# One core, four layers: the first layer's norm moves into its attention block, the first batch's experts move into the second batch, and the second layer's outputs go to two column groups

## The chip, the cores and the metric

The kernel runs on one core of a Trainium2 chip. The metric is the device time of one launch in microseconds (us); lower is better. The engines are TensorE (PE; PEld is its weight loading), VectorE (DVE), ScalarE (ACT), GpSimd (POOL) and SyncE (SP), which here only issues DMAs. Engines run their own instruction lists in order and meet at semaphores.

## The reference, cut to what matters

Eight batches of 512 tokens, 128 features, fp32, pass through four layers. Each layer is an attention-like mix followed by a feed-forward part. The change touches layers 0 and 1.

```
# layer 0: x -> norm -> xn; attention and experts both read xn, both are added to x
q, k = rms_norm(xn @ Wq, q_scale), rms_norm(xn @ Wk, k_scale)        # 16 heads of 8, mean over each head
attn = softmax(q @ k.T * hd ** -0.5);   o = (attn @ v) @ Wproj + bproj
logits = xn @ gate_w.T + gate_b                                      # 10 experts, 8 of them true
weights = top 2 of softmax(logits), null experts dropped, renormalised
y = sum over e of weights[e] * (xn @ expert_w[e]) + weights[e] * expert_b[e]

# layer 1: linear attention with decay, S_t = decay * S_(t-1) + k_t v_t, out_t = q_t S_t, then @ Wo.T + bo
# and experts chosen by a threshold of 0.9 on the summed probabilities, with a capacity per expert
```

## The kernel before, in words

Activations lie feature by token: `x` and `xn` are [128, 4096], batch b is the columns b*512 to b*512+511. Each part of a layer is one block, and a block ends with a barrier of all engines.

**The first norm** is a block of its own (`layer0_norm`, L306). SP loads the constants, `x` in two halves and the first weights. For each batch PE takes the mean (L225), DVE centres (L243), ACT squares (L254), PE takes the variance (L229), ACT takes logarithm and exponent for the reciprocal root (L258, L260) and DVE scales (L247). The attention block starts when all eight batches are normed.

**Layer 0's attention block** (`layer0_mix`, L396). A ring of three PSUM slots of two banks each (`ring_order0`) carries nearly all products; its order is that in which PE fills and others empty them. The code before the loop makes q and k of batch 0 (L745), their squares on POOL (L483), head means (L759) and roots on ACT (L492 to L500), scales and splits them on DVE (L576 to L582), copies them into stacks (`replicate` L771 on PE, `take_rep` L597 on DVE), and computes the gate's logits of all 32 token tiles (L271, 10 columns each). Then come 8 batches of 16 steps. In a step s PE makes four heads' scores (L783), ACT takes the exponent of 2 x 1024 columns (L527), and PE multiplies the probabilities of two steps earlier by v (`times_v`, L797). In between PE does for the next batch: q and k at step 2 (`project`), v at 5, head means at 7, `replicate` at 14 and 15; for the batch before: `place` at step 3 (numerators and denominators, L806) and `output` at 6 (L825). DVE empties the products: `copy_o(b, g)` (L604) after every fourth `times_v`; `take_nd` (L616) and two `divide` (L621, L625) after `place`; `weigh(b, e)` (L612) multiplies `xn` by the weight row of expert e for PE's `expert(b, e)` (L816). A batch's eight experts run in its steps 8 to 15, `expert_bias` (L821) last; batch 0's run in steps 13 to 15.

**Routing in layer 0.** DVE reads the logits (`route_start`, L634), ACT exponentiates, DVE normalises (`route_probs`), compares all pairs (`precedence`, L301, 19 instructions) and forms the weights (`route`, L652 to L667). PE turns them (`turn_cw`, L843, at step 6 of batch 0), DVE copies them (`store_rows`, L672), SP writes them to DRAM (L466), waits for that, and reads the eight rows of a batch back, each broadcast to 128 partitions (`cwb`, 2 MB, L473, and `cwT`, L474). For a further batch SP waits until the last `weigh` of the batch before and its `expert_bias` are done, since `cwb` has one buffer.

**Layer 1's attention block** (`layer1_route_and_attend`, L929). Per batch PE projects (L991, L992), computes states (L1020), transposes (L1000, L1001), products within chunks (L1011) and outputs (L1032, L1036: four matmuls of 128 columns and seven of 64, into 64 partitions of one bank). ACT copies the output (L1109), POOL decays it (L1188). At the same time DVE finds the capacity's thresholds in nine steps (L1261 to L1270), each of which needs a sum from PE (`add_up`, L1050); these stand in PE's list twice a batch from batch 3 on, and the first one needs the ranks that PE turns after batch 1's outputs (`turn`, L1044).

## Time and profile before

| what | value |
|---|---|
| time, median of 3 runs | 1760.14 us (1757.15 to 1762.73) |
| the profiled execution, its own time | 1764.6 us |
| its span from first to last instruction | 1762.8 us |
| busy share of the span | PE 96%, PEld 58%, DVE 56%, ACT 47%, POOL 23% |
| TensorE clock granted, mean | 0.969 of full |
| first norm's block | 0 to 27 us |
| layer 0's attention block | 27 to 428 us |
| layer 1's attention block | 428 to 527 us |

In a row of the timeline the first number is the start in us from the span's start, the second the length in us, then engine, line, operation, what it writes and reads, and how many instructions are merged (x4). In brackets stands how long the engine was idle before it and what ended that. An fp32 matmul is two instructions. Where a row merges several, its length is that of all.

### The profile page before, as it was taken

The page shows a single profiled execution, that of the slowest core. Times are in us where ns is not written, and L with a number is a line of the kernel's source. Part 1 is how long each engine was busy: PE and PEld are TensorE (multiplying, and loading weights), DVE is VectorE, ACT ScalarE, POOL GpSimd, SP SyncE. Part 2 cuts the span into 40 slices and gives each one's busy share as a digit, 9 for nine tenths or more (in the row PEclk, how much of TensorE's full clock was granted, in tenths as well). Part 3 has the DMA queues.
Part 4 walks back from the last instruction along what each step waited for, and adds up shares of the span by engine and source line. Part 5 has one row for each costly group of instructions (what it writes and reads, how often), then busy time and mean ns, then how long its engine had stood idle before and what let it go on. Part 6 is the DMA issues. An engine that isn't in the chain of part 4 may idle for free. (4 is left out here: it accounts for less than half of the span.)

```text
span 1762.8 us, 22855 instructions
## 1 busy us (share of the span) xinstructions
PE 1686.9 (96%) x8670; PEld 1014.9 (58%) x8670; DVE 994.3 (56%) x1650; ACT 837.2 (47%) x1047; POOL 411.6 (23%) x333
## 2 busy tenths in 40 slices
PE   7899999999999999999999999999999997999997
PEld 4332222223555557877778786877778773444443
DVE  4555555543665454455555454455554446888886
ACT  5667777776435543343344343343434334445442
POOL 1000000000563222030211202020211205655562
PEclk8699999999799999999999999999999998999998
DMA  2222222222008510000000000000000010000000
GB/s 80 50 51 49 49 49 49 49 49 112 15 7 187 156 38 1 1 1 2 1 2 1 1 1 1 1 1 1 1 1 1 1 59 1 7 7 7 6 12 12
DMA packets 20266, 49.24 MB, mean 28 GB/s; under 512 B 1024, under 2 KB 1792, under 8 KB 19392
## 3 DMA queue, kind: packets, MB, share of 16 engines
q1 hardware_dynamic: 20160, 47.79, 11.2%
q8 instruction: 70, 1.15, 0.3%
q14 instruction: 36, 0.29, 0.1%
HBM read 45.30 MB, written 2.36 MB: 27 GB/s over the span
## 5 line engine op out<-in xcount | busy, mean ns | idle before, releaser
L527 ACT ACTIVATE probs<-ps 128x1024 f32<-128x1024 f32 x256 | 245.8, 1024 | 87.6 <-PE ps L783 84.5
L1956 PEld LDWEIGHTS ps_o<-v,probs 128*128 128x128 f32 x2048 | 235.3, 192 | 31.0 <-issue 25.2
L1956 PE MATMUL ps_o<-v,probs 128*128 128x129 f32 x2048 | 248.1, 278 | 1.8 <-ACT probs L1684 1.2
L1684 ACT ACTIVATE probs<-ps_ring 128x1024 f32<-128x1024 f32 x128 | 127.0, 1024 | 212.2 <-PE ps_ring L1937 211.9
L1762 DVE TENSOR_REDUCE negmax<-ps_o 128x2 f32<-128x1024 f32 x64 | 78.5, 1226 | 136.9 <-PE ps_o L1912 136.9
L797 PE MATMUL ps<-probs,v 128*32 128x512 f32 x1024 | 139.0, 617 | 0.8 <-DVE o_sb L604 0.8
L1677 ACT ACTIVATE xn<-ps_ring,pack 128x512 f32<-128x512 f32 x64 | 40.5, 685 | 164.0 <-PE ps_ring L1524 164.0
L2151 POOL TENSOR_TENSOR rs<-r,state 128x512 f32<-128x512 f32 x64 | 85.5, 1337 | 93.7 <-DVE state L2306 93.7
L783 PEld LDWEIGHTS ps<-q_stack,k_stack 32*128 32x128 f32 x512 | 32.0, 186 | 123.2 <-issue 100.3
L1775 DVE RECIPROCAL rden<-ps_o 128x2 f32<-128x2 f32 x128 | 21.5, 168 | 143.8 <-PE ps_o L1956 143.8
L2306 DVE TENSOR_TENSOR_SCAN state<-decay,state,kv 128x511 f32<-128x511 f32 x64 | 98.5, 1539 | 6.9 <-issue 1.6
L1634 POOL TENSOR_TENSOR gate_low<-xn,gate_high 128x512 fp32r<-128x512 f32 x32 | 41.6, 1301 | 220.6 <-DVE gate_high L1755 220.6
L1524 PE MATMUL ps_ring<-gate_high,w_low 128*128 128x512 f32 x208 | 87.0, 418 | 1.8 <-DVEq L1738 1.4
L783 PE MATMUL ps<-q_stack,k_stack 32*128 32x512 f32 x512 | 81.5, 510 | 6.0 <-ACT probs L527 3.7
L1762 DVE TENSOR_REDUCE negmax<-ps_ring 128x2 f32<-128x1024 f32 x64 | 75.4, 1221 | 14.9 <-PE ps_ring L1912 14.9
L483 POOL TENSOR_TENSOR sq<-qk 128x1024 f32<-128x1024 f32 x8 | 15.2, 1895 | 293.8 <-DVE qk L565 293.8
L1524 PE MATMUL ps_ring<-gate_high,w_high 128*128 128x512 f32 x208 | 82.0, 394 | 0.0
L1524 PE MATMUL ps_ring<-gate_low,w_high 128*128 128x512 f32 x208 | 81.9, 394 | 0.0
L1387 DVE TENSOR_TENSOR hs<-h,score 128x512 f32<-128x512 f32 x64 | 47.4, 741 | 53.0 <-PE ps_y L1424 36.3
L816 PE MATMUL ps<-xe,pack 128*128 128x512 f32 x128 | 72.1, 652 | 5.4 <-DVE xe L612 5.4
L1524 PE MATMUL ps_ring<-xh,w_low 128*128 128x512 f32 x168 | 71.1, 423 | 3.9 <-POOL xl L1631 3.9
L1782 DVE SCALAR_TENSOR_TENSOR att<-ps_o,rden,att 128x128 f32<-128x128 f32 x224 | 68.4, 347 | 8.7 <-issue 0.4
(410 smaller groups left out, 3467.5 us busy)
## 6 DMA issues: line engine op xcount, KB each, us to landing
cwb<-combine_by_expert SPq DMA_DIRECT2D x8, 2048.0 KB
score<-score_by_expert SPq DMA_DIRECT2D x15, 1024.0 KB, 7.8
pack<-pack_dram SPq DMA_DIRECT2D x1, 3840.0 KB, 15.1
pack<-pack_dram SPq DMA_DIRECT2D x1, 2507.0 KB, 8.8
x<-x_in SPq DMA_DIRECT2D x2, 1024.0 KB, 6.1
out<-x SPq DMA_DIRECT2D x8, 256.0 KB, 2.0
pack<-pack_dram SPq DMA_DIRECT2D x1, 1479.0 KB, 6.4
pack<-pack_dram SPq DMA_DIRECT2D x1, 1140.0 KB, 9.4
```

The lines of the kernel that those rows point to most:

```text
L527: nc.scalar.activation(probs[n % 3][:, 2 * half:2 * half + 2, :], ps, ACT.Exp, scale=float(HD0) ** -0.5).then_inc(read, 1)
L783: last = nc.tensor.matmul(ps[:, k, :], single(stacks["k"][b % 2][rows, g, m * P:(m + 1) * P]), single(stacks["q"][b % 2][rows, g, :]), sta ...
L797: last = nc.tensor.matmul(ps_o[32 * j:32 * j + 32, :], v[b % 2][:, m, 4 * g + j, :], probs[n % 3][:, j, :], start=(m == 0), stop=(m == NBL ...
L816: nc.tensor.matmul(ps_y[:, :], w["expert0"][:, e * P:(e + 1) * P], xe[:, n % 3, :], start=(e == 0), stop=False).then_inc(xe_used, 1)
L1387: nc.vector.tensor_tensor(hs[:, n % 3, :], h[:, n % HS1, :], score[half % 3][:, i, :], ALU.mult).then_inc(hs_ready, 1)
L1524: last = nc.tensor.matmul(out, single(lhsT), single(rhs), start=(start and n == 0), stop=(stop and n == 2))
L1684: nc.scalar.activation(probs[:, n % 2, m, :, :], ps, ACT.Exp).then_inc(read, 1)
L1762: nc.vector.reduce_max(negmax[:, n % 2, :, m], ps[:, :, :], AX_X, negate=True).then_inc(read, 1)
L1782: last = nc.vector.scalar_tensor_tensor(att[:, m, :], o[:, k, 0:D], rden[:, i, k:k + 1], att[:, m, :], ALU.mult, ALU.add)
L1956: last = nc.tensor.matmul(ps_o[:, i, k * (D + 1):(k + 1) * (D + 1)], probs[:, (b * PAIRS + p) % 2, m, j, queries], v[:, m, h, :], start=(m ...
L2151: nc.gpsimd.tensor_tensor(rs[:, j % 4, :], r[:, b % 2, :], st[:, j, :], ALU.mult).then_inc(rs_ready, 1)
L2306: nc.vector.tensor_tensor_scan(st[:, j, 1:T], decay[:, b % 2, 0:T - 1], kv[:, j % 2, 0:T - 1], st[:, j, 0:1], ALU.mult, ALU.add).then_inc( ...
```

## The change

- `layer0_norm` is gone. Its steps run inside `layer0_mix`, in five groups of batches: 0, 1, 2 and 3, 4 and 5, 6 and 7 (`GROUPS0`). Their PSUM products go through the ring, the centred values into buffers of the probabilities. PE's list holds the last groups' steps between those of batch 0's attention, and the gate's logits are computed group by group, the last two groups' in steps 1 and 2 of batch 0.
- ACT does the roots of the head means of batch 0 (`first_rms`) before the squares and roots of groups 3 and 4.
- Routing on DVE stands later in batch 0: `route_start` behind `take_qk(1)`, the rest behind `copy_o(0, 0)`. `turn_cw` is at step 11 instead of 6.
- Batch 0's experts run on PE in steps 0 to 4 of batch 1, two in each of the steps 0 to 2, one in each of 3 and 4, then `expert_bias(0)`. DVE's `weigh(0, e)` stand between its other steps of batch 1, the last two behind both `divide(0)`.
- In layer 1 the outputs of the token columns 256 to 511 go to partitions 64 to 127, so that an output is [128, 256]. ACT's copy and POOL's decay work on that form, two POOL memsets (L1181, L1196) are gone, and `unproject` is two matmuls of 256 columns with their own weights.

```diff
-def layer0_norm(nc, sh):
...
+ROUTED_AT = 5
+GROUPS0 = ((0,), (1,), (2, 3), (4, 5), (6, 7))
...
@@ scalar
+            for g in range(3):
+                first_square(g)
+                first_root(g)
             act.wait_ge(bound_ready, 1)
             first_rms(0)
             first_rms(1)
-            act.wait_ge(exp_in, 1)
-            nc.scalar.activation(lg[:, :, :], lg[:, :, :], ACT.Exp).then_inc(exp_out, 1)
+            first_square(3)
+            first_square(4)
+            first_root(3)
+            first_root(4)
...
@@ vector
+            first_centre(0)
+            first_centre(1)
+            first_scale(0)
+            first_centre(2)
+            first_scale(1)
+            dve.wait_ge(sh["w_loaded"][0], 16)
+            bounds()
             take_qk(0)
+            first_centre(3)
+            first_scale(2)
             take_v(0)
...
             take_rep(0, 1)
-            route_start()
+            first_scale(3)
+            first_scale(4)
             for b in range(B):
                 follows = b + 1 < B
+                if b == 1:
+                    weigh(0, 0)
+                    weigh(0, 1)
                 take_rep(b, 2)
-                if b == 0:
-                    route_probs()
+                if b == 1:
+                    weigh(0, 2)
                 take_rep(b, 3)
-                if b == 0:
-                    precedence(nc, dve, lg, first, E0)
+                if b == 1:
+                    weigh(0, 3)
                 if b:
                     copy_o(b - 1, 3)
+                if b == 1:
+                    weigh(0, 4)
+                    weigh(0, 5)
...
                 if b:
                     take_nd(b - 1)
                     divide(b - 1, 0)
                     divide(b - 1, 1)
+                if b == 1:
+                    weigh(0, 6)
+                    weigh(0, 7)
...
@@ tensor
+            first_mean(0)
+            first_mean(1)
+            first_variance(0)
+            first_mean(2)
+            first_variance(1)
+            normed(0)
             project(0, 0)
             project(0, 1)
+            first_mean(3)
+            first_variance(2)
             project_v(0)
-            gate_logits(nc, xn, w["gate0"], ps_y, E0, range(0, 10))
             mean_square(0, 0)
             mean_square(0, 1)
-            gate_logits(nc, xn, w["gate0"], ps_y, E0, range(10, NT)).then_inc(logits_done, 1)
+            first_mean(4)
+            logits(0)
+            logits(1)
+            first_variance(3)
+            logits(2)
...
             replicate(0, 1)
+            first_variance(4)
...
-                    if s == 6 and b == 0:
+                    if b == 0 and s in (1, 2):
+                        last = logits(2 + s)
...
+                    if b == 0 and s == 11:
                         turn_cw()
                     if b and s == 3:
                         place(b - 1, 0)
                         place(b - 1, 1)
+                    if b == 1 and s < 5:
+                        if s == 0:
+                            pe.wait_ge(route_dve, ROWS)
+                        for e in ((0, 1), (2, 3), (4, 5), (6,), (7,))[s]:
+                            expert(0, e)
+                        if s == 4:
+                            expert_bias(0)
...
@@ layer 1, tensor
-                for m in range(NBLK):
-                    nc.tensor.matmul(ps[0:DS, BANK_O, m * P:(m + 1) * P], kv[:, b % 2, m, DS:2 * DS], inside[:, b % 2, m, :],
-                                     start=True, stop=False)
...
+                for first in range(NBLK // 2):
+                    for half in range(2):
+                        m = first + half * NBLK // 2
+                        nc.tensor.matmul(ps[half * DS:(half + 1) * DS, BANK_O, first * P:(first + 1) * P], kv[:, b % 2, m, DS:2 * DS],
+                                         inside[:, b % 2, m, :], start=True, stop=False)
```

How the lists stand at the three places that matter. PE, step 3 of batch 1, before (L806 is `place(0)`, L797 `times_v`, L783 the scores of step 4; `xe` are the weighed inputs):

```order
L806 MATMUL ps<-o_sb,pack 32x512 [waits o_copied,ring0_read1]
L806 MATMUL ps<-o_sb,pack 32x512 x3
L797 MATMUL ps<-probs_2,v 32x512 [waits ring0_read0,ring0_read2]
L797 MATMUL ps<-probs_2,v 32x512 x3
L783 MATMUL ps<-q_stack,k_stack 128x512 [waits ring0_read2]
```

The same place in the changed kernel (L847 is `place(0)`, L857 `expert`, L838 `times_v`, L824 scores, L862 `expert_bias`):

```order
L847 MATMUL ps<-o_sb,pack 32x512 [waits o_copied,ring0_read2]
L847 MATMUL ps<-o_sb,pack 32x512 x3
L857 MATMUL ps<-xe,pack 128x512 [waits xe_ready]
L838 MATMUL ps<-probs_2,v 32x512 [waits ring0_read1,ring0_read0]
L838 MATMUL ps<-probs_2,v 32x512 x3
```

An expert's matmul, which waits for DVE's `xe_ready`, now stands directly behind `place(0)`. DVE at the same place, before (L616 is `take_nd(0)`, L621 and L625 the two `divide(0)`, L604 `copy_o`):

```order
L616 COPY nd<-ps 128x1024 [waits ring0_done1]
L621 RECIPROCAL rden<-nd 128x256
L625 TENSOR_TENSOR on<-nd,rden 128x256
L621 RECIPROCAL rden<-nd 128x256
L625 TENSOR_TENSOR on<-nd,rden 128x256
L604 COPY o_sb<-ps 128x512 [waits ring0_done1,pv_done]
```

and in the changed kernel (L621 is now `weigh`, L625 `take_nd`, L630 and L634 `divide`, L613 `copy_o`, L580 `take_v`):

```order
L625 COPY nd<-ps 128x1024 [waits ring0_done2]
L630 RECIPROCAL rden<-nd 128x256
L634 TENSOR_TENSOR on<-nd,rden 128x256
L630 RECIPROCAL rden<-nd 128x256
L634 TENSOR_TENSOR on<-nd,rden 128x256
L621 TENSOR_TENSOR xe<-xn,cwb 128x512 [waits xe_used] x2
L613 COPY o_sb<-ps 128x512 [waits ring0_done2,pv_done]
L580 COPY v<-ps 128x64x8 [waits pv_done,ring0_done1]
L621 TENSOR_TENSOR xe<-xn,cwb 128x512 [waits xe_used,cw_loaded]
```

The input that PE's expert waits for, `weigh(0, 6)`, stands behind the copy and the two divisions, which themselves wait for `place(0)`. PE ahead of the first scores of batch 0, before (L745 the second of q and k, L752 v, L271 logits, L759 head means, L771 `replicate`):

```order
L745 MATMUL ps<-xn,pack 128x512
L752 MATMUL ps<-pack,xn 128x128 x4
L271 MATMUL ps<-pack,xn 128x10 x10
L759 MATMUL ps<-sq,pack 128x512 [waits squared] x2
L271 MATMUL ps<-pack,xn 128x10 x22
L771 MATMUL ps<-qk_high,sel 128x512 [waits ring0_read0,split_ready,padded,sel_ready]
```

and in the changed kernel (L800 head means, L894 `first_mean`, L901 `first_variance`, L272 logits, L812 `replicate`):

```order
L800 MATMUL ps<-sq,pack 128x512 [waits squared,ring0_read0] x2
L894 MATMUL ps<-x,pack 128x512 [waits ring0_read1]
L894 MATMUL ps<-x,pack 128x512
L272 MATMUL ps<-pack,xn 128x10 [waits norm0_dve]
L272 MATMUL ps<-pack,xn 128x10 x3
L272 MATMUL ps<-pack,xn 128x10 [waits norm0_dve]
L272 MATMUL ps<-pack,xn 128x10 x3
L901 MATMUL ps<-xn,pack 128x512 [waits norm_taken,ring0_read2]
L901 MATMUL ps<-xn,pack 128x512
L272 MATMUL ps<-pack,xn 128x10 [waits norm0_dve]
L272 MATMUL ps<-pack,xn 128x10 x7
L812 MATMUL ps<-qk_high,sel 128x512 [waits ring0_read0,split_ready,padded,sel_ready]
```

The variance of group 3, which waits for ACT's square (`norm_taken`), now stands ahead of `replicate(0, 0)`.

## Rows read from the trace of the kernel before

**Rows 1.** Busy time by stretch: PE, PEld, DVE, ACT, POOL, clock, DMA share, GB/s.

```profile
99.00:145.00 46.00, 44.83 (x264) 14.04 (x264) 23.88 (x29) 34.72 (x36) 1.90 (x1) 1.00 0.27 47
```

**Rows 2.** Timeline of PE from the first norm to batch 0's step 2.

```profile
6.35 6.06 PE L225 MATMUL n_ps<-x,pack 128*128 128x512 f32 x8 [6.35 <-DMA x<-x_in]
...
27.36 3.75 PE L745 MATMUL ps<-xn,pack 128*128 128x512 f32 x4 [3.68 <-PEq L309]
...
37.36 9.40 PE L271 MATMUL ps<-pack,xn 128*128 128x10 f32 x44
...
57.36 3.78 PE L745 MATMUL ps<-xn,pack 128*128 128x512 f32 x4 [0.32 <-DVE k_stack L597]
```

**Rows 3.** Timeline of DVE and ACT in the same stretch.

```profile
14.96 0.69 DVE L247 TENSOR_TENSOR xn<-n_xc,xn  x1
...
37.67 0.69 ACT L492 ACTIVATE inv<-ps,bound 128x512 f32<-128x512 f32 x1 [9.07 <-PE ps L759]
...
42.69 0.63 ACT L500 ACTIVATE inv<-inv 128x512 f32<-128x512 f32 x1
...
63.29 5.61 ACT L527 ACTIVATE probs<-ps 128x1024 f32<-128x1024 f32 x6 [5.18 <-PE ps L783]
```

**Rows 4.** One stretch of two us in batch 0, columns as in group 1.

```profile
78.00:80.00 2.00, 0.93 (x4) 0.28 (x2) 0.64 (x1) 1.88 (x3) 0.00 (x0) 0.86 1.00 146
```

**Rows 5.** Timeline of DVE: routing of layer 0, to `copy_o(0, 0)`.

```profile
57.22 4.77 DVE L301 TENSOR_TENSOR cwb<-logits 128x320 f32<-128x320 f32 x19
...
69.45 0.68 DVE L604 COPY o_sb<-ps 128x512 f32<-128x512 f32 x1
```

**Rows 6.** Timeline of SP, then DVE: the weights' way through DRAM.

```profile
71.09 1.27 SPq L466 DMA_DIRECT2D combine_by_expert<-cw_rows  x2
74.31 0.40 SPq L473 DMA_DIRECT2D cwb<-combine_by_expert  x1
...
89.38 1.90 DVE L612 TENSOR_TENSOR xe<-xn,cwb 128x512 f32<-128x512 f32 x3 [1.55 <-DMA cwT<-combine_by_expert]
```

**Rows 7.** Timeline of PE: experts, bias, and `times_v` of step 14.

```profile
95.42 2.84 PE L816 MATMUL ps<-xe,pack 128*128 128x512 f32 x6
...
102.85 1.12 PE L821 MATMUL ps<-cwT,pack 8*128 8x512 f32 x2
...
105.79 1.07 PE L797 MATMUL ps<-probs,v 128*32 128x512 f32 x8
```

**Rows 8.** Timeline of PE and of DVE: `place(0)` and the end of `divide(0)`.

```profile
113.18 1.92 PE L806 MATMUL ps<-o_sb,pack 128*32 128x512 f32 x16
...
120.48 0.43 DVE L625 TENSOR_TENSOR on<-nd,rden 128x256 f32<-128x256 f32 x1
```

**Rows 9.** Second load of weights: SP's issue, a stretch, PE from step 4 to 8.

```profile
104.06 0.40 SPq L473 DMA_DIRECT2D cwb<-combine_by_expert  x1
...
118.00:119.00 1.00, 0.58 (x6) 0.51 (x5) 0.93 (x3) 1.00 (x2) 0.00 (x0) 1.00 0.14 39
...
116.33 1.06 PE L797 MATMUL ps<-probs,v 128*32 128x512 f32 x8
...
126.84 1.12 PE L816 MATMUL ps<-xe,pack 128*128 128x512 f32 x2
```

**Rows 10.** Timeline of layer 1's attention block: PE, DVE, ACT, POOL.

```profile
460.43 0.43 PE L1032 MATMUL ps<-inside,kv 128*64 128x128 f32 x2
...
463.25 1.12 PE L991 MATMUL ps<-xn,pack 128*128 128x512 f32 x2
...
472.76 0.22 DVE L1261 TENSOR_SCALAR_CACHE_REDUCE n_cand<-pack,n_small 128x7 f32<-128x7 f32 x1
...
515.35 0.48 DVE L1272 TENSOR_SCALAR_CACHE_REDUCE n_prk<-n_rkT,n_small 128x256 f32<-128x256 f32 x1
...
524.89 0.59 ACT L1109 ACTIVATE o_raw<-ps 64x512 f32<-64x512 f32 x1 [3.00 <-PE ps L1036]
...
525.56 1.25 POOL L1188 TENSOR_TENSOR attended<-o_raw,d_o 64x512 f32<-64x512 f32 x1 [2.81 <-ACT o_raw L1109]
```

More of the change, by code:

```diff
@@ L698, in _ @@
                     divide(b - 1, 1)
+                if b == 1:
+                    weigh(0, 6)
+                    weigh(0, 7)
+                if b == 0:
+                    take_v(b + 1)
                 copy_o(b, 0)
-                if follows:
+                if b and follows:
                     take_v(b + 1)
```

222 lines of the change are left out of this document (124 added, 98 removed).

## The prediction

> **What bounds the kernel now.** I first read the busy shares by stretch. In the batches of layer 0, TensorE is busy 44.8 of 46.0 us at the full clock, ScalarE 34.7 [rows 1], and the next batch repeats it. So in layer 0 a wait of PE is lost time, and work can be moved but not hidden. Then I read the start on the timelines of PE, DVE and ACT. PE takes its first mean at 6.35 us and makes q and k of batch 0 only at 27.36, behind the barrier [rows 2]. From there to the second projection, which ends at 61.1, PE is nearly always busy too, but at the low clock of 1.2 GHz: two matmuls of 512 columns take 3.75 us [rows 2], where six expert matmul instructions (three matmuls) take 2.84 at the high clock [rows 7]. The 22 small logits matmuls take 9.40 us, 0.43 each [rows 2]. The first exponents behind that stretch start at 63.29 [rows 3]. The third view is the path of the expert weights: from the first write issued at 71.09 to the first `weigh` at 89.38 it takes 18.3 us [rows 6]. In layer 1 DVE's nine steps run from 472.76 to 515.35 [rows 10], in step with PE.
>
> **The start.** The chain mean, centre, square, variance, root, scale of batch 0 ends in the kernel before at 14.96 + 0.69 = 15.65 [rows 3]; in the new order it has fewer instructions ahead of it, so I take 14.5 for the first projection, 12.9 earlier. What follows is walked with the lengths of the rows. q and k, two means, two variances and v are dense and keep the clock high; the head means end at about 23.2 (projection 1.7, copy of q and k behind `bounds` and `scale(1)` to 19.4, squares on POOL to 21.4, 1.7). ACT's eight root steps of batch 0 take 42.69 + 0.63 - 37.67 = 5.65 us [rows 3], so 23.5 to 29.1. The square of group 3 stands behind them on ACT and takes about 1.0 (an exponent of 1024 columns is 5.61 / 6 = 0.94 [rows 3]): 30.1. PE has taken its mean of group 4 and eight logits tiles by 26.8 and then waits 3.3 us for that square, with nine further products queued behind it, `replicate` among them. I expect the clock to fall there, as it does at 78 to 80 us, where PE is busy 0.93 of 2.0 us and the granted clock goes to 0.86 in the mean [rows 4]. Then everything goes at the low clock. Variance 3: 3.4 (two matmuls, as the 3.75 less the tail). Eight logits tiles: 8 x 0.43 = 3.4. `replicate`: 1.9. Variance 4: 3.4, to 42.2. The roots of group 4 on ACT, two of 1024 columns, end at 45.0, and only then come the first exponents. Steps 1 and 2 bring the other 16 logits tiles (6.9 us), scores and copies, and the second projection (3.4): it ends at 60.0, its first `times_v` at 61.7. The exponents of step 3 start at about 62.2 instead of 63.29 [rows 3]. The 12.9 us won are spent: PE must do the norm's last ten matmuls and all logits in this stretch at the low clock, where before the norm ran at the high one.
>
> **Routing.** `route_probs` and the comparisons now follow `copy_o(0, 0)`, which can't be before `times_v(3)`, 68.5. From the first comparison to the copy behind the routing it took 69.45 - 57.22 = 12.2 us [rows 5]; one copy leaves this stretch, three small steps join it, which I set equal. So `copy_o(0, 1)` ends at 82.4. `times_v(8)` needs it at about 80.5 and waits some 2 us. `turn_cw` stands behind the scores of step 11: `times_v` 1.07 [rows 7], scores 0.5 and transposes 0.44 at twice that, with the hand-overs 4.6 us, so the rows are stored at 87.0 and, by the 18.3 us of [rows 6], the first `weigh` starts at 105.4 and the first expert matmul at 106.2. PE comes to it at 104.5, since steps 12 to 15 are light: **wait A**, 1.7 us.
>
> **Batch 1.** In the kernel before `times_v(14)` starts at 105.79 with all experts of batch 0 done [rows 7]. Now it follows two experts: 106.2 + 1.9 + 2.0 for the low clock = 110.1, **+4.3**. Six experts at 2.84 / 3 = 0.95 and the bias at 1.1 [rows 7] remain: **+6.8**. `weigh(0, 3)` and `weigh(0, 4)` stand behind a copy that itself waits for PE: about 1 us each, **+2.0**.
>
> **Wait B** is in step 3. `expert(0, 6)` stands directly behind `place(0)`. Its input comes behind `take_nd` and two divisions, which end at 120.48 + 0.43 = 120.91; `place` lets PE go on at 114.9 [rows 8]. With a `weigh` of 0.65 PE starts again at 121.6: 6.7 us, in which the kernel before did the scores and `times_v` of three steps. Behind such a gap I expect the low clock for a while: 1.5 us, between 0 (it doesn't fall) and 3.4 (four matmuls of 512 columns run in 7.5 instead of 3.8 us, as in [rows 2] against [rows 7]): **+8.2**.
>
> **Wait C** is in step 8. The weights of batch 1 are loaded after `expert_bias(0)`. In the kernel before the issue at 104.06 lands at about 118.5, where the DMA share falls to 0.14 [rows 9], 14.6 us after the bias. Then come `weigh(1, 0)`, `weigh(1, 1)` and `add(0)`, 2.2 us, before `expert(1, 0)` may start: 16.8. From `times_v` of step 4 to `expert(1, 0)` PE has 126.84 - 116.33 = 10.5 us of work [rows 9]. Before, the bias was at the end of batch 0 and the load was covered; now 6.3 us stick out. With 1.5 for the clock (bounds as for B): **+7.8**.
>
> **Layer 0** in sum: 4.3 + 6.8 + 2.0 + 8.2 + 7.8 = +29.1. Batches 2 to 7 are unchanged.
>
> **Layer 1.** The output products of a batch take 463.25 - 460.43 = 2.8 us [rows 10]. If pairs in two column groups overlap fully, they take 1.5; if not at all, 2.8. The nearest row is `times_v`, four column groups of 512 columns, eight instructions in 1.07 us [rows 7], where one matmul without groups takes 0.95: near full overlap, so I take 1.65, a gain of 1.15. The Trainium skill, page "TensorEngine Tiling (Array Packing)", section "Instruction Overhead", says that a matmul costs about 60 cycles however few columns it has, so that one should not take tiles from a dimension that is small already. By that the seven matmuls of 64 columns would gain nothing and the sum below would be about 1.3 us smaller; no row of before shows such pairs. Two outputs stand ahead of `turn`: -2.3. The nine steps take 42.6 us [rows 10]; DVE alone with PE's answer needs 4.26 a step, 38.3; I take 40.4, since one stretch of low clock will still be in it: -2.2. Behind the last step the last output saves 1.15 on PE, 0.25 on ACT (0.59 [rows 10], half the columns) and 0.5 on POOL (1.25 [rows 10]): -1.9. In all **-6.4**, with -1.5 and -9 as ends. The removed memsets and the new form of `unproject` cost nothing: POOL waits for tables there, and PE streams as many columns. Layers 2 and 3 keep their lengths.
>
> **Sum.** +29.1 - 6.4 = +22.7. The profiled run took 1764.6 us, 1.8 of it outside the span; with the change 1787. The median is 4.5 below, so 1760.1 + 22.7 = 1783.
>
> **Rivals.** (1) *The clock comes back for a part of the start*, at variance 3 or 4, and logits and `replicate` run at up to twice the speed. The first expert comes up to 5 us earlier, 1777. For it speaks that both variances are dense; against it that 9.40 us of logits in [rows 2] did not bring it back. (2) *The clock stays high through the start.* The first scores are then at 37, step 3 at 49, routing ends at 68.5, the first expert is at 91.2 (72.1 + 18.3 + 0.8), while PE comes to it at 82 and waits 9 us, which the load through DRAM sets. `times_v(14)` is at 94.6, -11.2; with 6.8 + 2.0 + 8.2 + 7.8 - 6.4 it is +7.2, 1767. It needs a clock that survives 3.3 us of waiting between small matmuls. (3) *Faster than before:* the high clock as in (2), and it also survives the waits, so that B and C cost 6.7 and 4.0 with the small waits inside them, and layer 1 gives its full 9: -12.7 + 6.8 + 6.7 + 4.0 - 9.0 = -4.2, 1756. The place is PE between 30 and 50 us; it decides when step 3's exponents start before 50 us and no low stretch follows `place(0)`. (4) *Layer 1 loses the clock.* With shorter outputs PE waits for DVE's counts twice a batch, and each low stretch costs about 3 us on a path where DVE had no slack. Two or three of them turn -6.4 into +3: 1792. (5) *The pairs don't overlap*: layer 1 gives only 1.5, 1788.
>
> **How the numbers follow.** Main case with (5) as its upper edge: 0.62, 1776 to 1791. (1) 0.16, (2) 0.08, (3) 0.05, (4) 0.09. The main case and (1) and (4) lie from 1775 to 1793; some of (2) is taken in for a range of 1767 to 1792. About 0.3%, 5.3 us, is what a measurement can tell from no change. Slower by more than that: main, (1), (4) and most of (2), 0.89 less a margin for a misread wait, 0.87. Within: rest of (2) and parts of that margin, 0.06. Faster: 0.07.
>
> **What would show it.** In the new profile: first projection near 14.5; PE waiting near 27 to 30 us for ACT's square; clock low from there to about 60; first exponents at 45, step 3's at 62; first `weigh` of batch 0 at 105; PE idle about 6.7 us behind `place(0)` with DVE's `xe` as the releaser; PE idle about 6 us before `expert(1, 0)`, DVE waiting for the DMA; layer 0's block ending near 457 instead of 428; outputs of a layer-1 batch in 1.65 us; that block some 6 us shorter. The prediction is wrong if the step-3 exponents start before 55 us, if PE goes on behind `place(0)` in under 3 us, or if the second load lands before PE's step 8.

## The result and the profile after

The changed kernel takes 1789.5 us (median of 4 runs, 1783.9 to 1790.4) against 1760.4 us of the kernel before on the same chip. The ratio is 1.015 (95% interval 1.0124 to 1.0176): slower by 29 us, where 1783 was forecast. The profiled execution took 1790.4 us, its span is 1788.3 us, 25.5 more than before; the mean granted clock is 0.965 instead of 0.969.

The start. Timelines of PE and ACT in the changed kernel (L901 is `first_variance`, L786 `project`, L536 the exponents of the scores, L504 `first_square`):

```profile
30.91 3.75 PE L901 MATMUL ps<-xn,pack 128*128 128x512 f32 x4 [3.43 <-ACT xn L504]
...
57.18 3.57 PE L786 MATMUL ps<-xn,pack 128*128 128x512 f32 x4
...
62.28 3.77 ACT L536 ACTIVATE probs<-ps 128x1024 f32<-128x1024 f32 x4 [6.50 <-PE ps L824]
```

The same stretch by windows (start:end, length, busy PE, PEld, DVE, ACT, POOL, granted clock, DMA share, GB/s):

```profile
26.00:28.00 2.00, 1.48 (x14) 1.38 (x13) 1.80 (x2) 1.85 (x4) 0.00 (x0) 1.00 0.00 0
28.00:30.00 2.00, 0.00 (x0) 0.00 (x0) 1.27 (x3) 1.86 (x4) 0.00 (x0) 0.93 0.00 0
30.00:32.00 2.00, 1.09 (x2) 0.60 (x3) 1.72 (x3) 1.71 (x2) 0.00 (x0) 0.50 0.00 0
...
43.00:46.00 3.00, 1.72 (x9) 0.49 (x8) 0.13 (x1) 2.34 (x3) 0.00 (x0) 0.94 0.00 0
46.00:60.00 14.00, 13.08 (x48) 9.44 (x48) 3.57 (x3) 5.54 (x6) 0.00 (x0) 0.53 0.01 1
```

PE waits 3.43 us for ACT's square of group 3, the clock falls to its low level within that wait, comes back for about 3 us at 43, and is low again to 60. Step 3's exponents start at 62.28, one us before the 63.29 of [rows 3]: the 12 us that the norm gained are gone.

Batch 0's experts. Timeline of DVE, SP and PE in the changed kernel (L621 `weigh`, L681 `store_rows`, L460 the load of the weights, L857 `expert`, L847 `place`, L862 `expert_bias`; L613 and L638 are `copy_o` and `add`):

```profile
85.74 0.43 DVE L681 COPY cw_rows<-ps 128x256 f32<-128x256 f32 x1 [3.47 <-PE ps L884]
88.94 0.40 SPq L460 DMA_DIRECT2D cwb<-combine_by_expert  x1
103.84 1.29 DVE L621 TENSOR_TENSOR xe<-xn,cwb 128x512 f32<-128x512 f32 x2 [7.64 <-DMA cwT<-combine_by_expert]
104.68 3.71 PE L857 MATMUL ps<-xe,pack 128*128 128x512 f32 x4 [7.35 <-DVE xe L621]
...
112.27 1.12 PE L857 MATMUL ps<-xe,pack 128*128 128x512 f32 x2 [0.93 <-DVE xe L621]
115.80 1.98 PE L857 MATMUL ps<-xe,pack 128*128 128x512 f32 x4 [0.98 <-DVE xe L621]
...
128.16 0.42 DVE L634 TENSOR_TENSOR on<-nd,rden 128x256 f32<-128x256 f32 x1
128.50 1.29 DVE L621 TENSOR_TENSOR xe<-xn,cwb 128x512 f32<-128x512 f32 x2
129.25 2.08 PE L857 MATMUL ps<-xe,pack 128*128 128x512 f32 x2 [6.46 <-DVE xe L621]
...
136.93 0.40 SPq L460 DMA_DIRECT2D cwb<-combine_by_expert  x1
151.62 1.29 DVE L621 TENSOR_TENSOR xe<-xn,cwb 128x512 f32<-128x512 f32 x2 [9.92 <-DMA cwT<-combine_by_expert]
153.64 2.07 PE L857 MATMUL ps<-xe,pack 128*128 128x512 f32 x2 [6.95 <-DVE x L638]
```

These are waits A (7.35), the two small ones (0.93, 0.98), B (6.46, behind the last divide) and C (6.95, behind the second load). The first expert matmul of 512 columns behind B and behind C takes 2.1 us, the two behind A 3.71, and one behind a small wait 1.1: the clock is low behind each long wait. The last row's place in the kernel before is 126.84, so the lag there is 26.8 us. Layer 1's block starts 28.3 us later than before; first the row of before, then that of after:

```profile
428.09 1.10 PE L1061 MATMUL ps<-x,pack 128*128 128x512 f32 x2 [0.94 <-PEq L396]
```

```profile
456.40 1.10 PE L1146 MATMUL ps<-x,pack 128*128 128x512 f32 x2 [0.94 <-PEq L365]
```

Layer 1. PE's timeline around two of the nine steps (L1115 and L1121 the output products, L1135 `add_up`, L1072 and L1073 projections, L1101 states):

```profile
505.14 0.44 PE L1115 MATMUL ps<-inside,kv 128*64 128x128 f32 x4
505.51 0.44 PE L1121 MATMUL ps<-qv,state 64*64 64x64 f32 x6
505.88 0.44 PE L1115 MATMUL ps<-inside,kv 128*64 128x128 f32 x4
506.25 0.45 PE L1121 MATMUL ps<-qv,state 64*64 64x64 f32 x8
507.74 0.59 PE L1135 MATMUL ps<-n_count,pack 128*128 128x7 f32 x2 [1.04 <-DVE n_first L1343]
508.19 2.06 PE L1072 MATMUL ps<-xn,pack 128*128 128x512 f32 x2
...
514.99 0.39 PE L1135 MATMUL ps<-n_count,pack 128*128 128x7 f32 x2
...
519.24 0.39 PE L1135 MATMUL ps<-n_count,pack 128*128 128x7 f32 x2 [1.04 <-DVE n_first L1343]
...
523.49 0.39 PE L1135 MATMUL ps<-n_count,pack 128*128 128x7 f32 x2 [0.17 <-DVE n_first L1343]
```

The output products take 1.5 us (505.14 to the end of the fourth row) where [rows 10] has 2.8. PE then waits 1.04 us for DVE's count, and what follows runs at the low clock: from one `add_up` to the next it takes 7.25 us (507.74 to 514.99) where the undisturbed distance is 4.25 (514.99 to 519.24). A low stretch costs 3.0 us here. From the first to the last `add_up` it takes 39.8 us (503.49 to 543.31) against 38.0 before, and the whole block from its first matmul to `unproject` 97.4 (456.40 to 553.81) against 99.15 (428.09 to 527.24). What is behind it is 1.1 us shorter than before, which nothing in the change explains.

### The profile page after: what moved, and what is told of

Same layout as the page of the kernel before. It is cut to its first block and busy times, and to the rows that moved or that the text cites. A ratio compares the mean times of both kernels' runs of the same rounds, so it can differ in the third digit from the quotient of the medians.

```text
span 1788.3 us, 22778 instructions
## 1 busy us (share of the span) xinstructions
PE 1682.0 (94%) x8686; PEld 1009.3 (56%) x8686; DVE 994.7 (56%) x1644; ACT 832.4 (47%) x1037; POOL 404.9 (23%) x331
## 5 line engine op out<-in xcount | busy, mean ns | idle before, releaser
L536 ACT ACTIVATE probs<-ps 128x1024 f32<-128x1024 f32 x256 | 246.2, 1024 | 121.9 <-PE ps L824 119.4
L838 PE MATMUL ps<-probs,v 128*32 128x512 f32 x1024 | 139.3, 618 | 4.6 <-DVE o_sb L613 4.6
L857 PE MATMUL ps<-xe,pack 128*128 128x512 f32 x128 | 76.5, 684 | 26.8 <-DVE xe L621 19.8
L824 PEld LDWEIGHTS ps<-q_stack,k_stack 32*128 32x128 f32 x512 | 31.1, 186 | 120.6 <-issue 97.0
L470 POOL TENSOR_TENSOR sq<-qk 128x1024 f32<-128x1024 f32 x8 | 15.1, 1892 | 349.0 <-DVE qk L574 349.0
L824 PE MATMUL ps<-q_stack,k_stack 32*128 32x512 f32 x512 | 78.5, 507 | 4.3 <-ACT probs L536 3.5
L613 DVE COPY o_sb<-ps 128x512 f32<-128x512 f32 x32 | 22.0, 688 | 93.2 <-PE ps L838 93.2
```

What stands on the lines that cost most here:

```text
L536: nc.scalar.activation(probs[n % 3][:, 2 * half:2 * half + 2, :], ps, ACT.Exp, scale=float(HD0) ** -0.5).then_inc(read, 1)
L824: last = nc.tensor.matmul(ps[:, k, :], single(stacks["k"][b % 2][rows, g, m * P:(m + 1) * P]), single(stacks["q"][b % 2][rows, g, :]), sta ...
L838: last = nc.tensor.matmul(ps_o[32 * j:32 * j + 32, :], v[b % 2][:, m, 4 * g + j, :], probs[n % 3][:, j, :], start=(m == 0), stop=(m == NBL ...
L857: nc.tensor.matmul(ps_y[:, :], w["expert0"][:, e * P:(e + 1) * P], xe[:, n % 3, :], start=(e == 0), stop=False).then_inc(xe_used, 1)
```

## Experiments

The table gives for each kernel the ratio to the kernel before, timed on the same chip, with its 95% interval, and from its profiled execution: the start of step 3's exponents (ACT), of the first expert matmul, of layer 1's block, the time from the first to the last `add_up`, and the length of layer 1's block up to `unproject`, in us.

| kernel | ratio | step 3 | first expert | layer 1 starts | nine steps | layer 1 |
|---|---|---|---|---|---|---|
| before | 1 | 63.3 | 90.2 | 428.1 | 38.0 | 99.2 |
| after | 1.015 [1.0124, 1.0176] | 62.3 | 104.7 | 456.4 | 39.8 | 97.4 |
| outputs_alone | 0.9985 [0.9969, 1.0001] | 59.2 | 86.2 | 424.0 | 37.2 | 93.3 |
| fill_counts | 0.9965 [0.9939, 0.9992] | 63.6 | 90.4 | 428.4 | 37.3 | 93.7 |
| layer0_only | 1.0159 [1.0124, 1.0193] | 61.5 | 103.9 | 455.6 | 38.1 | 102.3 |
| weigh_early | 1.0091 [1.0071, 1.0111] | 58.8 | 101.4 | 443.5 | 39.7 | 97.4 |
| split_load | 1.0053 [1.0037, 1.0070] | 62.2 | 99.3 | 438.9 | 38.2 | 95.7 |
| experts_back | 1.0059 [1.0040, 1.0079] | 62.3 | 105.2 | 442.9 | 39.7 | 97.5 |
| squares_first | 1.0135 [1.0118, 1.0152] | 59.6 | 102.0 | 452.2 | 38.2 | 97.4 |
| fill_start | 1.0110 [1.0084, 1.0135] | 56.8 | 99.3 | 451.0 | 35.7 | 93.4 |
| waits_away | 0.9999 [0.9979, 1.0018] | 59.8 | 96.9 | 430.0 | 35.4 | 96.2 |
| all_together | 0.9970 [0.9953, 0.9987] | 55.4 | 92.3 | 425.6 | 34.0 | 91.4 |
| all_more | 0.9954 [0.9935, 0.9974] | 54.7 | 91.7 | 423.3 | 34.0 | 93.4 |

Read the columns with care: `before`, `outputs_alone` and `fill_counts` have the same layer 0, and it ends at 428.1, 424.0 and 428.4; `after`, `weigh_early`, `split_load`, `experts_back` and `layer0_only` have the same start, and step 3 begins between 58.8 and 62.3. One profile's clock is worth up to 4 us in the start alone. The stretch from the first expert to layer 1's block is steadier: the three kernels with the old layer 0 take 337.8 to 337.9 us for it, and `after`, `layer0_only` and `fill_start` 351.7 each. But `squares_first`, with the same code in this stretch, takes 350.3, so a difference there says something from about 1.5 us on.

### Wait B: the order on DVE

```diff
+                if b == 1:
+                    weigh(0, 6)
+                    weigh(0, 7)
                 if b:
                     take_nd(b - 1)
                     divide(b - 1, 0)
                     divide(b - 1, 1)
-                if b == 1:
-                    weigh(0, 6)
-                    weigh(0, 7)
```

> The changed kernel with DVE's weigh(0, 6) and weigh(0, 7) ahead of take_nd(0) and the two divide(0) instead of behind them; nothing else differs. Theory (wait B is DVE's order, as the prediction says): PE's 6.46 us wait behind place(0) goes, and the low clock behind it (126 to 135 us) with it; the bias and so the second load start earlier by the same amount, and wait C stays as long: 6.5 to 8 us faster than the changed kernel, about 1782. Rival 1: wait C grows by what B loses (the load's start is not set by B): 0 to 1 us. Rival 2: output(0) at step 6 becomes late, since the divides end 1.3 us later: a new wait there, 4 to 5 us faster only.

PE in `weigh_early`, from `place(0)` to `expert(1, 0)`:

```profile
117.78 1.92 PE L847 MATMUL ps<-o_sb,pack 128*32 128x512 f32 x16
119.63 1.13 PE L857 MATMUL ps<-xe,pack 128*128 128x512 f32 x2
120.69 1.06 PE L838 MATMUL ps<-probs,v 128*32 128x512 f32 x8
...
128.24 1.13 PE L866 MATMUL ps<-on,pack 128*128 128x512 f32 x2
...
140.92 2.07 PE L857 MATMUL ps<-xe,pack 128*128 128x512 f32 x2 [6.78 <-DVE x L638]
```

Wait B is gone, no wait came at `output(0)` (128.24), and wait C is as long as before (6.78). The ratio falls from 1.015 to 1.009, about 10 us. From the first expert to layer 1's block it takes 342.1 us instead of 351.7 (443.49 - 101.41, 456.40 - 104.68): 9.6 us for a wait of 6.46, so the low clock behind it costs some 3 in the changed kernel's execution, twice what I took. Rivals 1 and 2 are out.

### Waits A and C: the load

```diff
...
+                for half in range(2):
+                    if b:
+                        sp.wait_ge(xe_ready, b * E0_TRUE - 4 + 4 * half)
+                    sp.dma_start(cwb[:, 4 * half:4 * half + 4, :], here[4 * half:4 * half + 4, :].unsqueeze(0).broadcast_to([P, 4, T])
+                                 ).then_inc(half_loaded[half], 16)
                 if b:
-                    sp.wait_ge(xe_ready, b * E0_TRUE)
...
-                sp.dma_start(cwb[:, :, :], here.unsqueeze(0).broadcast_to([P, E0_TRUE, T])).then_inc(cw_loaded, 16)
...
-                if e == 0:
-                    dve.wait_ge(cw_loaded, b * 32 + 32)
+                if e in (0, 4):
+                    dve.wait_ge(half_loaded[e // 4], b * 16 + 16)
...
```

> The changed kernel with the 2 MB of expert weights of a batch loaded in two halves on SP's queue (experts 0 to 3, then 4 to 7), each as soon as the four weigh that read the buffer half are done, and the cwT row load behind them. Theory (waits A and C are the load's length and its late start): the first half of batch 0 lands some 7 us earlier (about 96.5 instead of 103.8), so wait A of 7.35 us goes; the halves of batch 1 are issued at about 112 and 128 instead of 136.9, so wait C of 6.95 us goes too; B stays. 14 us faster than the changed kernel, about 1775. Rival 1: a half takes as long as the whole (latency, not bytes): A stays 7 us, C goes; about 1782. Rival 2: halves side by side slow down the others: 0 to 5 us.

DVE's first `weigh`, PE's first and seventh expert with the `times_v` behind it (L842), and SP's second load in `split_load` (its two halves in one row):

```profile
98.43 1.29 DVE L625 TENSOR_TENSOR xe<-xn,cwb 128x512 f32<-128x512 f32 x2 [2.37 <-DMA cwb<-combine_by_expert]
99.27 1.96 PE L861 MATMUL ps<-xe,pack 128*128 128x512 f32 x4 [2.10 <-DVE xe L625]
...
122.09 2.07 PE L861 MATMUL ps<-xe,pack 128*128 128x512 f32 x2 [6.46 <-DVE xe L625]
124.09 1.54 PE L842 MATMUL ps<-probs,v 128*32 128x512 f32 x8
...
105.08 17.93 SPq L461 DMA_DIRECT2D cwb<-combine_by_expert  x2
```

Wait C is gone, wait A is 2.10 instead of 7.35 (the first `weigh` comes 5.4 us earlier, not 7.3), and the experts behind A run at the high clock (1.96 for four instructions instead of 3.71). B stays at 6.46, but here the clock is back after 1.4 us of loss (2.07 and 1.54 instead of 1.12 and 1.06). The kernel is 17 us faster than the changed one where 14 was expected. In the profiled execution layer 1's block starts 17.5 us earlier: 5.4 up to the first expert, 12.1 behind it, and of these only 6.95 are wait C; the rest is the clock behind the waits. Both rivals are out.

### The experts back in batch 0

```diff
@@ vector
+                if b == 0:
+                    weigh(b, 0)
+                    weigh(b, 1)
+                    weigh(b, 2)
                 copy_o(b, 2)
...
@@ tensor
-                    if b == 1 and s < 5:
...
-                        for e in ((0, 1), (2, 3), (4, 5), (6,), (7,))[s]:
-                            expert(0, e)
...
+                    elif s >= 13:
...
+                        for e in ((0, 1), (2, 3, 4), (5, 6, 7))[s - 13]:
+                            expert(b, e)
...
```

> The changed kernel with batch 0's experts back in steps 13 to 15 of batch 0 (on PE and on DVE as in the kernel before, the bias in step 15); norm inside the block, late routing and the second layer's part stay. Theory (waits B and C come from moving the experts into batch 1, wait A from the late routing and the load): PE waits for the first expert at step 13, from about 93 to 104.5, 11 to 12 us, with the low clock behind it; waits B and C (13.4 us with up to 3 of clock) and the two small ones (1.9) are gone. Net 3 to 8 us faster than the changed kernel, about 1783. Rival: the wait at step 13 is longer than what it saves, since six experts' weigh steps hold up DVE's copy_o and take_rep for batch 1: same or slower than the changed kernel.

```profile
105.19 3.51 PE L850 MATMUL ps<-xe,pack 128*128 128x512 f32 x4 [15.35 <-DVE xe L621]
```

This row is PE's first expert in `experts_back`. PE waits 15.35 us for it, more than the 11 to 12 expected, and yet the kernel is 16 us faster than the changed one, not 3 to 8. The expectation set this wait against B, C and the small ones (13.4 + 3 + 1.9 us) and left out that wait A, 7.35 us, goes too: the first expert comes when the load lets it, at 105.19 here and at 104.68 in the changed kernel. From there to layer 1's block it takes 337.7 us, as in the kernel before (428.09 - 90.22 = 337.9).

So the 28.3 us of layer 0 split in two. What follows the first expert takes 13.9 us more (351.7 against 337.9), from the experts in batch 1, although three steps of batch 0 are already done by then. And the first expert comes 14.5 us later (104.68 against 90.22). Step 3 starts 1 us earlier, but SP issues the first write of the weights 15.1 us later (86.19 against the 71.09 of [rows 6]). DVE's comparisons in the changed kernel start 13.3 us later than the 57.22 of [rows 5]:

```profile
70.48 4.78 DVE L302 TENSOR_TENSOR cwb<-logits 128x320 f32<-128x320 f32 x19
```

That the late routing makes the first expert late is read from these times; no run puts the routing back by itself.

### The start

```diff
             act.wait_ge(bound_ready, 1)
+            first_square(3)
+            first_square(4)
             first_rms(0)
             first_rms(1)
-            first_square(3)
-            first_square(4)
```

> The changed kernel with ACT's squares of groups 3 and 4 ahead of the eight root steps of batch 0's head means instead of behind them. PE's 3.43 us wait before variance(3) at 27.5 us goes, but the roots and with them replicate come about 1.9 us later. Theory of the prediction (the clock falls behind that wait, at 30 us): the high clock lasts longer, variance(3) takes 1.9 instead of 3.75 us, and the step-3 exponents start 3 to 10 us before the 62.28 of the changed kernel; total 0 to 4 us faster or the same, since the load through DRAM and waits A and C stand. Rival: the clock falls all the same, because PE then waits for replicate's input with small logits matmuls ahead: step-3 exponents within 1 us of 62.3 or up to 2 us later, total within 2 us of the changed kernel.

PE in `squares_first` (L812 is `replicate`):

```profile
32.42 0.79 PE L812 MATMUL ps<-qk_high,sel 32*128 32x512 f32 x2 [2.17 <-DVE qk_low L591]
...
35.21 0.79 PE L812 MATMUL ps<-qk_high,sel 32*128 32x512 f32 x2 [1.57 <-DVE qk_low L591]
```

The wait of 3.43 us is gone and the clock stays at 1.00 until 30, but two waits, 2.17 and 1.57, stand at `replicate`, and the clock falls at the first. Step 3 starts at 59.6; `weigh_early`, with an unchanged start, has 58.8. The edit moved the wait, and nothing is shown of a gain.

```diff
             logits(1)
+            for _ in range(3):
+                nc.tensor.matmul(ps_o[:, :], sh["common"]["mean_all"], x[:, at(0)], start=True, stop=True)
             first_variance(3)
```

> The changed kernel with three additional matmuls of 512 columns (fp32, result in a bank that the attention's output overwrites later, used by nobody) ahead of first_variance(3), where PE otherwise waits 3.43 us for ACT's square. Their length at the high clock is 2.9 us, so they delay nothing. Theory (the low clock of 30 to 60 us comes from that wait): variance(3) runs in 1.9 us instead of 3.75, the granted clock stays at 1.00 past 30 us, and the step-3 exponents start several us before the 62.28 of the changed kernel; the total is 1 to 6 us lower, since the chain to the first expert shifts with them. Rival: the clock falls all the same within a few us, through the short logits matmuls and the waits around replicate: step-3 exponents within 1.5 us of before, total the same within 2 us.

The variances of groups 3 and 4 in `fill_start`, and two windows (columns as above):

```profile
29.87 1.95 PE L901 MATMUL ps<-xn,pack 128*128 128x512 f32 x4 [0.77 <-ACT xn L504]
...
34.74 3.44 PE L901 MATMUL ps<-xn,pack 128*128 128x512 f32 x4
```

```profile
32.00:34.00 2.00, 2.00 (x18) 1.89 (x19) 0.00 (x0) 1.92 (x2) 0.00 (x0) 1.00 0.03 8
34.00:36.00 2.00, 2.00 (x8) 0.93 (x5) 1.79 (x2) 0.11 (x1) 0.00 (x0) 0.58 0.00 0
```

With work in place of most of the wait the variance takes 1.95 us instead of 3.75 and the clock stays high to 34. Step 3 starts at 56.8, 2.0 us before the earliest of the five unchanged starts. So the wait did bring the low clock at 30: the variance takes 3.75 us in all five executions with the unchanged start and 1.95 or 1.96 in all three with the additional matmuls. But at 34 the clock falls without a wait over 0.77 us ahead, behind 1.8 us of logits matmuls of 10 columns and the first `replicate`, in which PE counts as busy all the time. Both theories hold for a part: the first fall comes from the wait, a later one needs none as long. These matmuls don't set the moment of the later fall either. `all_together` and `all_more`, below, have the same list on PE up to there; the variance of group 4 in each:

```profile
34.45 1.98 PE L905 MATMUL ps<-xn,pack 128*128 128x512 f32 x4
```

```profile
35.45 2.93 PE L905 MATMUL ps<-xn,pack 128*128 128x512 f32 x4
```

In `all_together` the clock is at 1.00 up to 40, in `all_more` it falls between 36 and 38. Of the 8.8 us by which the profiled execution of `fill_start` is shorter than that of the changed kernel, 5.4 are there at the first expert, and its layer 1 block happens to be 4 us shorter as well. How much of the 5.4 comes from the edit is not shown, since unchanged starts differ by 3.5 us among themselves. But step 3 starts earlier in all three executions with the additional matmuls (56.8, 55.4, 54.7) than in any of the five without.

### Layer 1

> The kernel before with only the second layer's part of the change (outputs in two column groups, [128, 256] copy and decay, two half-width unproject matmuls); layer 0 is that of before. Prediction on record: layer 1's block 6.4 us shorter (1.5 to 9), a median near 1754. Theory after reading the changed kernel's trace: the 11 output matmuls do fall from 2.8 to 1.5 us a batch, but PE then waits about 1 us for DVE's counts at every odd add_up, and the clock is low behind two or three of these waits, 3.0 us each (508.19 to 519.24 against 519.48 to 527.75 in the changed kernel): the block is only 0 to 3 us shorter, median 1757 to 1760. Rival (rival 4 of the prediction in full): the low stretches outweigh the gain, block longer, median over 1762. If the block is 5 us or more shorter here, the missing gain in the changed kernel comes from layer 0's shift and not from the second layer's part itself.

The block is 5.8 us shorter than before in the profiled execution (93.3 against 99.15), near the forecast of 6.4, not 0 to 3. The median says less, 0.9985. Every odd `add_up` waits 1.04 us, as in the changed kernel, but only two low stretches follow, each 1.4 us (distances of 5.66 instead of 4.25); behind the other two waits the clock stays high.

```diff
                 if b >= 3 and 2 * (b - 3) + 1 < STEPS1:
+                    if b < B:
+                        nc.tensor.matmul(ps[DS:2 * DS, BANK_K, :], w["wk1"], xn[:, at(b)], start=True, stop=True)
                     add_up(2 * (b - 3) + 1)
```

> outputs_alone with one additional matmul of 512 columns (fp32, 0.95 us at the high clock, into partitions that nobody reads) ahead of each odd add_up in layer 1, four in all, where PE waits 1.04 us for DVE's count. It adds work and removes none. Theory (the wait of 1.04 us brings the low clock, and a low stretch costs 3.0 us a batch; otherwise DVE's 4.25 us a step sets the pace): no low stretch is left in the nine steps, they take about 38.5 us, and the kernel is 1 to 5 us faster than outputs_alone although PE does 4 us more work. Rival (the low stretches come from the short matmuls, not from the wait): the low stretches stay, and the time is the same or up to 2 us longer.

PE in `fill_counts` (L1108 is the additional matmul, L1054 `add_up`, L1040 outputs):

```profile
485.93 1.07 PE L1108 MATMUL ps<-xn,pack 128*64 128x512 f32 x2
487.04 0.39 PE L1054 MATMUL ps<-n_count,pack 128*128 128x7 f32 x2
...
500.15 0.39 PE L1054 MATMUL ps<-n_count,pack 128*128 128x7 f32 x2 [0.52 <-DVE n_first L1264]
...
502.91 0.57 PE L1040 MATMUL ps<-qv,state 64*64 64x64 f32 x8
503.42 1.97 PE L1108 MATMUL ps<-xn,pack 128*64 128x512 f32 x2
```

While the clock is high the additional matmul costs nothing and the steps follow each other at 4.25 us. But at 503 the clock falls here too. The last wait ahead of that is one of 0.52 us, before 500.15, and what stands between are transposes and products of 64 columns. The nine steps take 37.3 us as in `outputs_alone`, so the theory, which had no low stretch left, missed. The two ratios, 0.9985 and 0.9965, can't be told apart. In `all_together` and `all_more` the same code keeps all eight distances at 4.25 us (34.0 in all), and none of the eight executions of the new form without the additional matmuls is below 35.4. That the matmuls make the low stretches rarer is likely from this and not shown, and what brings the low clock in this loop stays open.

> The changed kernel with the second layer's part undone (outputs in one column group, POOL's memsets and unproject as in the kernel before); layer 0 is that of the changed kernel. Theory (the parts add up, layer 0 costs 28 to 29 us, the second layer's part gave 1.7 us in the profiled run of the changed kernel because of its low clock): layer 0's block ends at 456 us, layer 1's block takes about 99 us as in the kernel before, and the ratio is 1.016 to 1.018. Rival (layer 1's part is worth its 5.8 us in the changed kernel too, and what was seen is one profile's clock): the ratio is 1.018 to 1.021.

The ratio, 1.0159, lies at the edge of the first theory, but its interval takes in both. Layer 0 ends at 455.6, as expected. Layer 1's block, in the old form, takes 102.3 us in this profile, 3.2 more than in the kernel before with the same code. Beside it the new form's 97.4 is a gain of 4.9; beside [rows 10]'s execution it is 1.7.

### Together

> The changed kernel with all three remedies: loads in halves, weigh(0, 6) and weigh(0, 7) ahead of take_nd(0), ACT's squares of groups 3 and 4 first. Theory (the three waits with their clock are the 29 us of layer 0, and add up): split_load was 17 us faster than the changed kernel and still has wait B of 6.46 us and its low clock; without it 24 to 27 us faster than the changed kernel, 1761 to 1765, so no faster than the kernel before. Rival 1: with the waits gone the norm's 12 us at the start come out as a gain: under 1757. Rival 2: the waits come back elsewhere (output(0), the second half's load): 1768 or more.

0.9999. Layer 1's block starts at 430.0 instead of 456.4, so the two lines on DVE, the load and the squares held back 26.4 of layer 0's 28.3 us; the kernel before has 424.0 to 428.4 there, and what is left is about made up by the second layer's part. The squares' share in it is not shown. No gain is behind the waits. Wait A is still 1.9 us.

`all_together` is split_load, weigh_early, fill_start and fill_counts in one; `all_more` adds two more matmuls of 512 columns in steps 0 and 1.

> The changed kernel with the loads in halves, weigh(0, 6) and weigh(0, 7) ahead of take_nd(0), the three additional matmuls ahead of first_variance(3) and the four ahead of the odd add_up. Theory: the parts add up. The first expert matmul comes at about 91.5 us (104.68 less 5.4 as in fill_start, less 6.8 to 7.7 as in split_load); from there to layer 0's block end 333 us as in waits_away; layer 1's block 93.5 as in fill_counts: span about 1753, ratio to the kernel before 0.994 to 0.997. Rival: what the fill matmuls save at the start is lost at the wait for the first expert, since the load's length sets it: as waits_away, ratio 0.998 to 1.002.

The first expert comes at 92.3 (forecast 91.5), layer 0 takes 333.3 us from there (333), and layer 1's block is 91.4 long (93.5); the span is 1750.9. In the median 0.997 [0.9953, 0.9987], as added up.

> all_together with two more additional matmuls of 512 columns in steps 0 and 1 of batch 0 (ahead of replicate(0, 2) and of the scores of step 1), where PE waits 0.77 and 1.32 us for ACT at 38 to 41 us. Theory (each wait of about 1 us among short matmuls brings the low clock down here too): the 12 us between 42 and 55 us run at the high clock, step-3 exponents and the first expert come 3 to 6 us earlier, ratio 0.991 to 0.995. Rival: the logits matmuls of 10 columns bring the low clock by themselves (in fill_start the clock fell at 34 us, behind a stretch without a wait over 0.8 us): no change against all_together, or up to 2 us longer.

PE in `all_more`, the two logits groups in steps 1 and 2:

```profile
43.84 1.95 PE L272 MATMUL ps<-pack,xn 128*128 128x10 f32 x16
...
46.16 3.23 PE L272 MATMUL ps<-pack,xn 128*128 128x10 f32 x16
```

One of the two groups runs at the high clock now (1.95 us, 3.59 in `all_together`), in the other the clock falls while it runs. Step 3 starts 0.7 us earlier, not 3 to 6. 0.9954 [0.9935, 0.9974] can't be told from `all_together`. Both are faster than the kernel before, by 0.3 to 0.5%; but so is `fill_counts`, which has no part of the norm's move in it. The change to layer 0, with every remedy, is not shown to be worth anything.

## Why the prediction was right, and where it was not

**The direction and the mechanism held.** Slower by 29 us, forecast 23, with the range up to 1792. Point by point, forecast first:

- *First projection* 14.5, measured 15.39. *PE's wait for the square* until 30.1, measured 30.91; *clock* low from there to 60, with a short return at 43 that I had not. *First exponents* 45.0 and 45.74. *Step 3* 62.2 and 62.28. Right for this execution; with the same start four others lie between 58.8 and 62.3, so a hit within 0.1 us is in part luck.
- *`copy_o(0, 1)` ends* 82.4, measured 82.27. The wait of `times_v(8)` was 3.55 instead of 2. *Rows stored* 87.0, measured 86.19 (SP's first write). *First `weigh`* 105.4, measured 103.84.
- *Wait A* was forecast at 1.7 us and is 7.35. PE came to it at 97.3, not 104.5: I had made steps 12 to 15 of batch 0 too long; between 88 and 100 the clock is at 1.00. It did not enter the sum wrongly, since the first expert's time hangs on the load alone (106.2 against 104.68), and `times_v(14)` came at 108.32 instead of 110.1. The term was +4.3 and is +2.5.
- *Small waits* 2.0, measured 0.93 + 0.98. *Wait B* 6.7, measured 6.46. *Wait C* 6.3, measured 6.95. The clock behind B was taken at 1.5 us; it cost about 3 in the changed kernel, by `weigh_early`, and 1.4 in `split_load`, both within the bounds of 0 to 3.4. Behind C the lag grows from 26.8 to 28.3, 1.5 as taken.
- *Layer 0* +29.1, measured +28.3. The terms that were too low (the clock behind B, wait C) and too high (`times_v(14)`) nearly cancel, which is luck.
- *Layer 1* -6.4, measured -1.7. **This term failed.** The output products take 1.5 us, even less than the 1.65 taken. The part ahead of `turn` gave 0.8 instead of 2.3, the tail behind the last step 2.4 instead of 1.9. The nine steps were to be 2.2 shorter and are 1.5 us longer, from DVE's first candidates (500.22, before 472.76) to the last sum. In the step "one stretch of low clock will still be in it" there were three (distances of 7.25, 5.65 and 5.66 us instead of 4.25, in all 5.8 us). Rival 4 named this mechanism; its size, +3, was not reached. Eight executions of this form have one to three such stretches, so the term was not to be had from one profile.
- *The median.* I took the offset of before's profiled execution, 4.5 us above its median, to hold for the changed kernel. There it is 0.9 us. That is 3.6 us of the miss. The three profiles of one and the same layer 0 in the table, 4 us apart, show why such an offset doesn't carry over.
- *The chances.* The main case, (1) and (4) make 0.87 by themselves; with most of the 0.08 of (2) the sum for slower is above 0.9 and not the 0.89 that stands there.

The sizes above make up the difference: 4.7 (layer 1) + 3.6 (median) - 0.8 (layer 0) - 1.1 (the rest of the kernel) = 6.4 us, and 1789.5 - 1783 = 6.5.

**The rivals.** (1), a clock that comes back for a part of the start: in the changed kernel's execution it came back only at 43, for 3 us. But in `weigh_early`, whose start is the same, it was back by 34 and until after 36, the variance of group 4 took 3.03 us instead of 3.73, step 3 began at 58.8 and the first expert came at 101.4, 3.3 us earlier. So (1) is not out: it is what one of five executions does. (2), high through the start, happened in none. (3), faster than before, needs what `all_together` does by force, waits B and C away, A down to 1.72 us and a high clock up to 40 and in layer 1, and even then the gain is 0.3%, no more than `fill_counts` has without the norm's move. (5), pairs that don't overlap, is out: 1.5 us. From start to next start the 14 instructions of 64 columns take 0.37 + 0.38 = 0.75 us in the changed kernel (the first of the two is 505.51 to 505.88 in the rows above) and 0.25 + 3 x 0.37 = 1.36 us in the kernel before. In the prediction I drew from the Trainium skill, page "TensorEngine Tiling (Array Packing)", section "Instruction Overhead", that these products would gain nothing. That was a wrong use of the page: it warns of making a small dimension smaller, and here each of these matmuls keeps its 64 columns; what is split is the side of the array that the outputs go to. The measured 0.75 against 1.36 us speaks against my use and leaves the page's rule untested.

**What stays open.** How much layer 1's part is worth in the median: two pairs of profiles say 4.9 and 5.8 us, one says 1.7, the medians 2.6 (outputs_alone, give or take 3) and 1.6 (after against layer0_only, give or take 8). What brings the low clock in layer 1's loop, and when it comes back in the start. How the 14.5 us up to the first expert would shrink with the routing in its old place. And why the rest of the kernel is 1.1 us shorter.

## What to carry to other kernels

Before moving work to where an engine has no slack, write down for every input of the moved instruction what stands ahead of its producer on that engine, and when its buffer comes free; here two lines on DVE and one load, with the squares on ACT whose share isn't shown, held back 26 us (`waits_away`). A load that is needed piece by piece is issued piece by piece. A wait on TensorE is priced with the low clock behind it, 1.4 to 3 us for waits of 6 to 7 us here, and a term that rests on the clock in a tightly coupled loop gets a range of both signs, worked out from several profiles if there are any.

## What the runs showed of the hardware

- A wait of 1.04 us on PE in a loop of short matmuls can be followed by a low stretch that costs 3.0 us, and doesn't have to: with the same code in layer 1 the nine steps took between 35.4 and 39.8 us. The Trainium skill, page "TensorE: Matmul & The Clock Gate", section "A second HAM failure mode: psum-queue depth-cycling", tells of a kernel whose clock goes to and fro because TensorE is idle for short times between groups of matmuls. The loop in layer 1 looks like that; that its short waits are the cause is not shown, since the clock fell in `fill_counts` with no wait over 0.52 us close ahead.
- The clock also fell where PE had counted as busy for some us: behind matmuls of 10 columns and `replicate` (`fill_start`, at 34 us, the last wait 0.77 us ending at 29.87) and behind transposes and products of 64 columns (`fill_counts`, at 503 us, the last wait 0.52 us ending at 500.15). With the same instructions it stayed high up to 40 us in `all_together`.
- The low clock behind one and the same wait of 6.46 us cost about 3 us in one kernel and 1.4 in another.
- Matmuls that nobody needs, four of 512 columns in layer 1 (1.07 us in the row above), cost nothing while the clock was high: the steps stayed 4.25 us apart. Three of them at the start took the length of the next four instructions from 3.75 to 1.95 us.
- With a 2 MB load in two halves DVE can start 5.4 us earlier than with the whole (98.43 against 103.84), which is 9.6 instead of 14.9 us after the issue (88.85 and 88.94), not half the time. The two halves were issued one right behind the other there.
